# Attention kernel on one core: the causal mask of the first 128 queries, as a TensorE product or inside VectorE's maximum

## What is computed

```python
h = tokens(x / 255.) @ W + b, class token, + pos_emb      # [64, 197, 192]
att = q @ k^T * 16 ** -0.5                                # 12 heads
att = where(causal, att, -inf); att = softmax(att)        # keys after the query are left out
h = layernorm(h + (att @ v) @ w_proj + b_proj)
h = layernorm(h + experts(h))                             # top 2 of 8, capacity 1.2 N / E
```

## Time and profile before

| | |
|---|---|
| median of 3 executions | 2321.46 us (2321.45 to 2325.84) |
| profiled execution | 2324.15 us |
| its span, first to last instruction | 2322.4 us |
| mean granted TensorE clock | 0.968 |
| busy, share of span: PE, PEld | 2134.6 (92%), 2068.0 (89%) |
| DVE, ACT, POOL | 1578.2 (68%), 1084.3 (47%), 1577.8 (68%) |
| L659 (mask product of S[0]), 400 to 1200 us | 246 times, 273 ns |
| L841, L844 (maxima), whole span | 384 times each, 421 and 556 ns |

### The profile page before, as it was taken

The page is one execution under the profiler, slowest core; times in us unless marked ns, Lnnn a source line. Parts: engine busy times, 40 slices in busy tenths (PEclk is TensorE's granted clock), DMA queues, the critical chain, the costliest instruction groups (busy, mean ns, idle before and its releaser), DMA issues. The chain is left out here.

```text
span 2322.4 us, 49007 instructions
## 1 busy us (share of the span) xinstructions
PE 2134.6 (92%) x14772; PEld 2068.0 (89%) x14772; DVE 1578.2 (68%) x4286; ACT 1084.3 (47%) x2850; POOL 1577.8 (68%) x2317
## 2 busy tenths in 40 slices
PE   5999999999999999999999479999999999999980
PEld 5999999999999999999988379999999999999980
DVE  5577777777777777777777446666666666665656
ACT  2444444444444444444444245454545445454545
POOL 3366767676767676767656657777777777777756
PEclk8999999999999999999999689999999999999995
DMA  7656565656565656565644143201010101001338
GB/s 204 144 132 146 132 145 130 145 129 145 129 145 130 142 130 142 128 144 128 144 97 99 32 107 56 42 5 29 4 31 5 30 5 29 4 4 24 56 44 334
DMA packets 235842, 223.54 MB, mean 96 GB/s; under 512 B 90647, under 2 KB 216066, under 8 KB 234688
## 3 DMA queue, kind: packets, MB, share of 16 engines
q1 hardware_dynamic: 135872, 147.40, 25.0%
q10 hardware_dynamic: 45568, 59.31, 11.2%
q0 software_dynamic: 54272, 15.20, 5.4%
HBM read 154.56 MB, written 98.38 MB: 109 GB/s over the span
## 5 line engine op out<-in xcount | busy, mean ns | idle before, releaser
L1159 POOL DMA_INDIRECT x_tokens<-yout,e_entry x240 | 383.6, 1598 | 182.5 <-DVE yout L1340 136.1
L668 PE MATMUL Y<-p,vp 128*102 128x198 f32 x1536 | 360.9, 344 | 14.8 <-ACT ysb L490 8.8
L1355 DVE TENSOR_TENSOR a<-UP,gate 128x384 f32<-128x384 f32 x320 | 178.5, 558 | 220.2 <-ACT gate L1295 214.7
L446 POOL DMA_INDIRECT expert_lists<-entry,slot x256 | 290.3, 1134 | 54.1 <-issue 54.1
L495 ACT ACTIVATE p<-ST 128x396 f32<-128x396 f32 x384 | 190.9, 497 | 261.3 <-PE ST L640 254.8
L1144 POOL DMA_INDIRECT rows<-x_wide,e_entry x240 | 249.5, 1040 | 78.8 <-issue 71.9
L1295 ACT ACTIVATE gate<-GT 128x384 f32<-128x384 f32 x320 | 157.8, 493 | 298.2 <-PE UP L1237 298.2
L141 POOL TENSOR_TENSOR word_p<-word_p 1x1 f32<-1x1 f32 x416 | 89.1, 214 | 294.0 <-ACT p L497 282.1
L412 POOL TENSOR_TENSOR x_lo<-x,x_hi 128x396 fp32r<-128x396 f32 x192 | 205.4, 1072 | 80.9 <-ACT x_hi L466 79.2
L668 PEld LDWEIGHTS Y<-p,vp 128*102 128x102 f32 x1536 | 221.7, 170 | 29.6 <-issue 8.8
L841 DVE TENSOR_REDUCE rm<-S 128x2 f32<-128x256 f32 x384 | 161.8, 421 | 106.5 <-PE S L659 104.0
(11 more groups left out here) (212 smaller groups left out, 6640.8 us busy)
## 6 DMA issues: line engine op xcount, KB each, us to landing
x<-in_xt ACTq DMA_DIRECT2D x180, 198.0 KB
q<-qk_features SPq DMA_DIRECT2D x384, 74.2 KB
k<-qk_features SPq DMA_DIRECT2D x192, 148.5 KB
qk_features<-qk_hi SPq DMA_DIRECT2D x96, 198.0 KB, 2.8
qk_features<-qk_lo SPq DMA_DIRECT2D x96, 198.0 KB, 3.8
rb<-rd ACTq DMA_DIRECT2D x128, 74.2 KB
t_x<-x_tokens SPq DMA_DIRECT2D x15, 576.0 KB, 8.2
out<-t_o ACTq DMA_DIRECT2D x15, 576.0 KB, 8.2
```

Source lines behind the costliest of these rows:

```text
L446: pool.indirect_dma_start(d["lists"][:, :], bass.IndirectOffsetOnAxis(ap=slot[o][0:REAL[t], t, c:c + 1], axis=0), entry[o][0:REAL[t], t, c ...
L668: return pe.matmul(Y[0:VW1, 0:TI], v0, p32[b][:, hh, 0:TI], start=start, stop=stop)
L1159: pool.indirect_dma_start(d["x1"][:, :], row_of(cc, t), yout[q][:], None, bounds_check=N - 1, oob_is_err=False, compute_op=ALU.add)\
L1355: dve.tensor_tensor(a32[m % 2][:], UP[m % 2][:, 0:TILE3], gate[m % 2][:], ALU.mult)\
```

## The change

The product of identity and mask into S[0] (L659) is left out; the one into S[1] (L658) stays and now signals s_s. DVE adds a mask in f32 (a new constant `later`, 128x128, one more load at the start) while it takes the maximum: one tensor_tensor_reduce for each of the two heads, with a discarded bf16 copy in `masked`. A word instruction carries the wait for the scores and one for the maxima of the step before. The new instruction can't negate its maximum, so both reductions keep the sign and the copy of the turned maxima on ACT multiplies by -1.

```diff
+LOW = -3.0e38
+        later, masked = sb("later", [P, P], F32), sb("masked", [P, 2, TI], BF16)
-        late_loads = [(bqk, "bqk"), (ident, "ident"), (masks, "masks"), (iota8, "iota8"), (kbase, "kbase"),
+        late_loads = [(bqk, "bqk"), (ident, "ident"), (masks, "masks"), (later, "later"), (iota8, "iota8"), (kbase, "kbase"),
...
-                            act.activation(nm[im][0:NH, :], src[0:NH, 0:TI], ACT.Copy)\
+                            act.activation(nm[im][0:NH, :], src[0:NH, 0:TI], ACT.Copy, scale=-1.0)\
...
                 pe.matmul(S[0][:, b * P:(b + 1) * P], qt[rows, im, b, j, 0:P],
-                          kt[rows, im, j, 0:P], start=(b == 0), stop=False)
+                          kt[rows, im, j, 0:P], start=(b == 0), stop=(b == 1))
...
-                pe.matmul(own, identb[0:T1, 0:T1], repeat(maskb[0:T1, 0:T1], 2), start=False, stop=True)
-                pe.matmul(S[0][:, 0:2 * P], identb, repeat(maskb, 2), start=False, stop=True).then_inc(s_s, 1)
+                pe.matmul(own, identb[0:T1, 0:T1], repeat(maskb[0:T1, 0:T1], 2), start=False, stop=True)\
+                    .then_inc(s_s, 1)
...
-                        dve.wait_ge(s_s, n + 1)
-                        dve.tensor_reduce(rm[im][:, 0, j:j + 7:6],
-                                          S[0][:, 0:2 * P].rearrange("p (h c) -> p h c", h=2),
-                                          AX.X, ALU.max, negate=True)
+                        words.wait((s_s, n + 1), (s_m, n))
+                        for b in range(2):
+                            col = b * (NH // 2) + j
+                            dve.tensor_tensor_reduce(
+                                out=masked[:, b, 0:P], in0=S[0][:, b * P:(b + 1) * P], in1=later[:],
+                                scale=1.0, scalar=LOW, op0=ALU.add, op1=ALU.max,
+                                accum_out=rm[im][:, 0, col:col + 1])
                         dve.tensor_reduce(rm[im][0:T1, 1, j:j + 7:6],
                                           S[1][0:T1, 0:TP].rearrange("p (h c) -> p h c", h=2),
-                                          AX.X, ALU.max, negate=True).then_inc(s_m, 1)
+                                          AX.X, ALU.max).then_inc(s_m, 1)
...
+    ins["later"] = np.where(n[None] > n[:, None], np.float32(-1e30), np.float32(0.0))
```

## The result

The changed kernel takes 2387.68 us (median of 4, 2384.79 to 2391.45) where the kernel before takes 2323.14 (median of 4 beside it). The ratio is 1.028, with a 95% interval of 1.026 to 1.030: slower by 64.5 us. The prediction of 2324.5 with a range of 2308 to 2348 was wrong.

What follows compares the result with a forecast made beforehand. PE sets the pace except at one spot per pair of images, where DVE's maxima do. Saving 0.07 us a step on PE and adding 0.42 on DVE leaves +0.09 a body, +2.8 in 31: 2324.5 us, range 2308 to 2348.

Steps and rivals of the forecast that it cites:

- The word costs 0.21: DVE's wait-carrying word ahead of the maxima: 0.21 us to the next instruction's start, from 599.97 to 600.18.
- What is added: DVE's part of the forecast: a word and two passes replace one reduction, 0.42 us a step, 161 us in all.
- costs nothing that I count: The word's second wait, on the maxima of the step before: met long before, so counted as no cost.
- The clock falls: Rival: PE's longer stall at step 7's first scores matmul lowers its clock once each body, +46 us, 2370; chance 0.05.
- head 5 to head 7: From step 5's first scores matmul to step 7's, set by DVE's sum: 4.35 us before, 5.08 forecast.
- X: DVE time from the word's start to the second reduction's start: 0.34 us before, 0.76 forecast, bounds 0.50 and 1.02.
- What bounds the kernel: PE sets the pace in ten of twelve steps; DVE's 4.35 us sum sets it before step 7's first scores matmul.
- head 8: Step 8's first scores matmul: 0.66 us later; PE's ysb wait takes up part, leaving 0.44 at step 9's.
- The passes: DVE's two 128x128 mask-and-maximum passes: 0.21 us each plus 0.06 to write out the maximum.
- The longer chain by slow passes: Rival: DVE's passes at two cycles an element or waiting read-outs, X 1.02, +28 us, 2349; chance 0.18.
- The slot: PE time saved per step by dropping the mask product: 0.07 us, 0.11 at most, since the next weight load takes 0.10.
- rival of the shorter chain: Rival: X of 0.50 on DVE and 0.11 us saved per step on PE, -17 us, 2304.5; chance 0.19 with wider slot.

Runs made afterwards that it cites:

- e1: The changed kernel with the word's second operand read from PSUM in place of SBUF: 2317.83 us, ratio 0.9975 to the kernel before.
- e2: The kernel before without the mask product into S[0] and nothing in its place, maxima over unmasked scores: 2303.93 us, ratio 0.9912.
- e3: The changed kernel with 12 extra matmuls into unused columns of ST[1] ahead of PE's wait in step 7: 2347.75 us, ratio 1.011.
- e5: The changed kernel with POOL's x_lo written as a one-operand copy of x, its wait in a POOL word: 2328.00 us, ratio 1.0014.
- e4: The kernel before with only the two-operand SBUF word added ahead of its reductions, mask product kept: 2383.44 us, ratio 1.0257.
- e8: The kernel before with a word ahead of its reductions whose second operand is in PSUM: 2327.69 us, ratio 1.0021.
- e6: The changed kernel without the word; S[1]'s reduction goes first and carries the waits, the second pass signals: 2324.06 us, ratio 0.9999.

## Why the prediction was wrong

The step that failed is "The word costs 0.21" in **What is added**, with "costs nothing that I count" for its waits. The word's price was read from one row, and what POOL runs at that moment was not looked at. That row was itself the end of a hold: the word at 599.97 in the earlier trace rows ends at 600.25, and POOL's timeline of the kernel before has beside it

```profile
599.22 1.01 POOL L412 TENSOR_TENSOR x_lo<-x,x_hi 128x396 fp32r<-128x396 f32 x1
```

which ends at 600.23. A word that met only the last 0.26 of x_lo was taken for the price of any word; the same word early in x_lo takes 0.96 to 1.20. The second step that failed is the rival **The clock falls**, held at 0.05 and at nothing in the sum. The hold at full clock is worth 18 us, which would have put the time near 2341, inside the range; the 46 us of the clock took it out. By the prediction's own sum, head 5 to head 7:

| | predicted | after | e1 |
|---|---|---|---|
| head 5 to the first word | 0.67 | 0.66 | 0.67 |
| X of step 5 | 0.76 | 0.50 | 0.49 |
| on to the word of step 6 | 2.27 | 2.31 | 2.36 |
| X of step 6 | 0.76 | 1.54 | 0.49 |
| on to head 7 | 0.62 | 0.61 | 0.61 |
| sum | 5.08 | 5.62 | 4.62 |

- **What bounds the kernel** was right: the wait sits at head 7, and the chain adds up to the hundredth in all three kernels. PE's wait was forecast at 35 to 45 us with about 1 us at head 7; it is 54.7 and 1.66, by the X of step 6. At head 8 the prediction let a wait for ACT's ysb take up part of the delay; its row, [0.16 <-issue] at 604.62, names no such wait, and that reading stays unproven.
- **The passes** were mis-sized the other way. Start to start 0.21, as taken; the read-out of the accumulator (73 ns) overlaps fully and costs 0, not 0.06; a free word starts its follower after 0.07 to 0.08, not 0.21. X is the lower bound of 0.50. The Trainium skill, "VectorE: DVE Perf Modes", section "Two Vector instructions with no wait between them", has the read of the accumulator as an instruction of its own. The rows agree, but it takes no time in the chain. The longer chain by slow passes did not come: 128 elements with a source in SBUF and one in PSUM take 0.27.
- **DVE's busy time** rose by 117 us (1578.2 to 1694.9), not 160, held words included.
- **The slot** is nearer to 0.11 than to 0.07: S[1]'s product and the next matmul are 0.07 apart (622.93 to 623.00), where they were 0.07 and 0.11 (596.05 to 596.12, 600.56 to 600.67 in the earlier trace rows). The argument on weight loads (0.10 behind L658) was wrong: the matmul starts 0.07 behind. e2 with its 20 us shows that more than half of these slots goes into waits for ACT, as the prediction said of them.
- **With the hold removed the sum has the right sign and too large a size.** X = 0.49 and the wider slot gave 2X - 1.67 = -0.69 a body, the narrow one -0.45; e1's ten heads 7 are 38.55 apart, -0.35, and the kernel is 6 us faster than before, where 31 times -0.69 is 21. The rival of the shorter chain (2304.5) had the mechanism and an optimistic size.
- **The clock rival** (0.05, 2370) was right that the clock can fall at head 7. That its 46 us are what the rows give (46; e3 gives 40) is luck: it took 1.5 us in every body behind a stall of 1.1, and measured are 2.9 us in about every second body behind a stall of 1.66. At stalls near 1.1 the runs don't bear it out: with 0.92 to 0.94 at head 7 (e5) the clock never falls between 400 and 1200, with 1.49 to 1.52 (e4) behind one of 19. It became likely only with the held word, and no case joined the two.

**Shown:** that the word's second SBUF operand is the cause (e1, e4, e8), that what POOL runs sets the length of the hold (e5, for x_lo), and that part of the loss is the clock (e3). **Not settled:** why the clock falls behind 11 of 19 heads 7 of the changed kernel and in e4, whose stalls of 0.59 and 1.49 are no shorter in sum, behind one of 19; and what holds words beside a DMA_INDIRECT.

The Trainium skill, "SBUF — State Buffer", section "Who interferes with whom", says that a VectorE instruction with two inputs in SBUF contends with a GpSimd instruction that reads SBUF. This case's rows agree: 1.20 us for one element beside x_lo, 0.14 with one operand in PSUM. By its words the instruction that issues first blocks the other. The row at 624.13 reads otherwise at first sight, since x_lo starts 0.17 after the word; but POOL was reading for L436 when the word started, and x_lo came next without a gap, so the word seems to have stood behind both (0.19 for the end of L436 and 1.01 for x_lo make the 1.20). That order is read from the rows and was not tested by itself. Nor do the starts say who is held. In the kernel before, x_lo starts at 597.17 and y, with two operands in SBUF, 0.08 later (597.25); y keeps its 0.35 and x_lo is the longer one, 1.31 in place of 1.01:

```profile
597.17 1.31 POOL L412 TENSOR_TENSOR x_lo<-x,x_hi 128x396 fp32r<-128x396 f32 x1
```

In step 3 of the changed kernel the word starts 0.08 behind x_lo as well, and there it is the word that is held.

## What to carry to other kernels

Before an instruction is added to a chain, look at what the other engine runs at that very moment of each period: a one-element addition cost 0.08 us or 1.1 depending on POOL (621.32 to 621.40, 624.13 to 625.25). An instruction of VectorE that only carries waits should have at most one operand in SBUF. And a stall of PE is priced twice, once as time and once by what the clock may do after it; filling it with useless matmuls shows the second part in one run. Before a product that masks is moved, ask whether what it masks needs the mask at all (e2).

## What the runs showed of the hardware that was not expected

- DVE's TENSOR_TENSOR on one element lasts 0.15 us alone, 0.96 or 1.20 when a 128x396 TENSOR_TENSOR of POOL starts within 0.2 us of it, 0.57 beside a CAST of the same size that starts 0.06 after it, and 0.14 whatever POOL does when one operand is in PSUM. The passes, one source in PSUM and one in SBUF, stay at 0.27 to 0.28 beside x_lo (46 of them wholly beside it in e1 between 400 and 1000).
- The mask-and-maximum pass of 128x128 holds DVE 0.21 us start to start, its accumulator's read-out 0. Behind a TENSOR_REDUCE of 396 elements it starts 0.47 to 0.49 after that one's start in 156 cases of e6 and 0.58 to 0.59 in 31.
- After a stall of 1.66 us PE ran at about half its clock (0.57 granted from 626 to 634) for 7 us in about every second body, which made a body 2.9 us longer; with the stall cut to 0.39 by 12 matmuls it kept 1.00.
